# Attention over fp16 halves with weight halves kept in memory, and an output half read one step earlier

## What is computed

```python
def _L0_attn_ref(x, Wq, bq, Wk, bk, Wv, bv, Wo, bo):
    q = proj(Wq, bq) * scale          # proj: x @ W + bias, split in 16 heads
    k = proj(Wk, bk)
    v = proj(Wv, bv)
    q = apply_rotary(pos, q)
    k = apply_rotary(pos, k)
    sim = jnp.einsum('bhid,bhjd->bhij', q, k)
    sim = jnp.where(causal, -jnp.finfo(sim.dtype).max, sim)
    attn = jax.nn.softmax(sim, axis=-1)
    out = jnp.einsum('bhij,bhjd->bhid', attn, v)
    out = out.transpose(0, 2, 1, 3).reshape(b, n, INNER)
    return out @ Wo + bo
...
x = _layernorm(x + _L0_attn_ref(...), axis=-1)
x = _layernorm(x + _L0_ffn_ref(...), axis=-1)
```

## Time and profile before

| | us |
|---|---|
| median of three runs | 1857.92 (1856.61 to 1859.83) |
| the profiled execution | 1852.92 |
| its span in the profile | 1851.1 |

### The profile page before, as it was taken

How to read it: one execution, slowest core, us unless ns; L and a number is a source line. 1 busy time by engine, 2 the same in 40 slices (tenths; PEclk the granted TensorE clock), 3 DMA queues, 4 the chain that set the end, 5 groups by cost and what they waited for, 6 DMA issues and landing times. The chain is left out here.

```text
span 1851.1 us, 33747 instructions
## 1 busy us (share of the span) xinstructions
PE 1755.6 (95%) x10464; PEld 1409.7 (76%) x10464; DVE 1564.9 (85%) x3748; ACT 1463.9 (79%) x2658; POOL 1394.8 (75%) x1293
## 2 busy tenths in 40 slices
PE   6899999999999999999999999999999999899997
PEld 4677877777777777777777777777777777668886
DVE  6788888888888888988888888888888889867886
ACT  5788888888888888888888888888888888754443
POOL 4688877778777878888778878787888877624554
PEclk9899999999999999999999999999999999989999
DMA  3756565666665666576666655675666765540001
GB/s 93 165 116 113 111 139 117 122 131 129 118 119 120 142 120 115 114 157 119 120 122 117 138 111 116 141 141 121 119 114 116 156 141 109 104 99 12 24 24 35
DMA packets 638257, 210.01 MB, mean 113 GB/s; under 512 B 609408, under 2 KB 622208, under 8 KB 636672
## 3 DMA queue, kind: packets, MB, share of 16 engines
q1 hardware_dynamic: 614400, 165.91, 47.9%
q10 hardware_dynamic: 23680, 41.95, 7.9%
HBM read 48.40 MB, written 8.39 MB: 31 GB/s over the span
## 5 line engine op out<-in xcount | busy, mean ns | idle before, releaser
L863 DVE SCALAR_TENSOR_TENSOR planes<-S,recip,planes 128x128 f16<-128x128 f32 (+7 forms) x512 | 417.5, 815 | 113.0 <-ACT planes L665 111.3
L656 ACT ACTIVATE S<-p_row,neg_max 128x128 f32<-128x128 f32 (+7 forms) x512 | 381.5, 745 | 138.9 <-DVE neg_max L853 138.8
L665 ACT ACTIVATE planes<-S,recip 128x128 f16<-128x128 f32 (+7 forms) x512 | 378.9, 740 | 101.4 <-DVE recip L914 73.7
L427 POOL TENSOR_TENSOR swap<-swap,sin_t 128x512 f32<-128x512 f32 x256 | 331.5, 1295 | 166.0 <-ACT swap L673 164.9
L853 DVE CUSTOM_DVE_ANT_0 p_row<-S,mask_row 128x128 f32<-128x128 f32 (+7 forms) x512 | 387.0, 756 | 27.0 <-PE S L1123 26.4
L421 POOL TENSOR_TENSOR rot<-rot,swap 128x512 f32<-128x512 f32 x252 | 325.5, 1292 | 53.6 <-DVE rot L904 50.7
L673 ACT ACTIVATE swap<-S,bqk 64x512 f32<-64x512 f32 x512 | 350.8, 685 | 18.6 <-PE S L1141 5.8
L1123 PE MATMUL S<-QKA 128*128 128x512 f32 (+4 forms) x1152 | 261.9, 354 | 10.3 <-DVE planes L863 5.7
L1123 PE MATMUL S<-QKB 128*128 128x512 f32 (+4 forms) x1152 | 260.4, 353 | 0.4 <-DVE planes L863 0.3
L1074 PE MATMUL O<-PT,VA 128*128 128x512 f16 (+3 forms) x1152 | 215.4, 328 | 29.0 <-issue 25.5
L1074 PE MATMUL O<-PT,VB 128*128 128x512 f16 (+3 forms) x1152 | 214.9, 327 | 29.4 <-issue 27.0
(11 more groups left out here) (134 smaller groups left out, 2955.5 us busy)
## 6 DMA issues: line engine op xcount, KB each, us to landing
w_raw<-in_w_heads ACTq DMA_DIRECT2D x64, 256.0 KB, 2.9
wv_raw<-in_w_heads ACTq DMA_DIRECT2D x32, 256.0 KB, 3.4
PT<-planes SPq DMA_TRANSPOSE x512, 3.4
wo_raw<-in_wo_heads ACTq DMA_DIRECT2D x32, 256.0 KB, 2.6
attn_d<-resid ACTq DMA_DIRECT2D x4, 1024.0 KB, 6.3
x_raw<-in_x_cols SPq DMA_DIRECT2D x3, 1024.0 KB, 5.9
resid<-in_x_rows ACTq DMA_DIRECT2D x3, 1024.0 KB, 5.3
resid<-in_x_rows SPq DMA_DIRECT2D x2, 1024.0 KB, 6.8
```

Of the source, the lines that this page charges most:

```text
L427: nc.gpsimd.tensor_tensor(swap[:, c, :], swap[:, c, :], sin_t[:, half], ALU.mult).then_inc(sin_done, 1)
L656: nc.scalar.activation(row_psum(n, s)[:, 0:cols], p_row[:, k % 2, 0:cols], ACT.Exp, bias=neg_max[:, s:s + 1], scale=-1.0, accum_out=row_su ...
L665: nc.scalar.activation(row_halves(n, s)[:, 0], row_psum(n, s)[:, 0:cols].rearrange("p (j q) -> p j q", q=P), ACT.Copy, scale=recip[:, s:s ...
L863: nc.vector.scalar_tensor_tensor(halves_of[:, 1], row_psum(n, s)[:, 0:cols].rearrange("p (j q) -> p j q", q=P), recip[:, s:s + 1], halves_ ...
```

## The change

- x, W, WV, QK, OT and WO become fp16 halves (`at(...)` places them by hand in one region, so that the later part's float32r operands can lie over them). Since fp16 has a narrow range, each gets a factor from a bound: x a factor per batch, W of each head, WV and WO of each pair. The maxima are VectorE's (`weigh_w`, `weigh_v`, `weigh_wo`), their sum over partitions is a matmul with ones read by `take_...`, and `scale_...` makes the factors and what undoes them: the biases `bqx`, the factor `to_score` of the masked maximum, which was the constant -SCALE, `v_up`, and `pv` of the addition into resid. The raw weights are multiplied by GpSimd before they are split.
- The halves of the weights of heads 0 to 15 are written to memory once (`keep_...` on SyncE), and from head 16 on they are loaded into `W`, `WV` and `WO` as they are (`load_..._halves`); weighing, copying and subtracting weights ends with head 15. At each change of batch the factors are renewed (`weigh_all`, `take_x`, `scale_x`, `scale_out`).
- `w_raw`, `wv_raw` and `wo_raw` have two buffers, `WV` and `WO` too. In heads 1 to 13 `w_high` stands in steps 1 and 2.
- `output_high` and `output_low` of the second half of O stand in step 6.
- The loads of resid and x and the stores of resid are cut into quarters, one or two to a step.

The core of the diff:

```diff
-    xT = sb("xT", [P, 2, KT, N], F32R)
...
+    xT = at(AT_X, "xT", [P, 2, KT, N])
+    W = [at(AT_W + 4096 * i, f"W{t}", [P, 2, 2, KT, P]) for i, t in enumerate("AB")]
+    WV = [at(AT_WV + 2048 * i, f"WV{t}", [P, 2, KT, 2, P]) for i, t in enumerate("AB")]
+    QK = [at(AT_QK + 16384 * i, f"QK{t}", [P, 2, 2, N]) for i, t in enumerate("AB")]
+    OT = [at(AT_OT + 8192 * i, f"OT{t}", [P, 2, N]) for i, t in enumerate("AB")]
+    V = [sb(f"V{s}", [P, 2, NT, 2 * P], F16) for s in "AB"]
+    WO = [sb(f"WO{s}", [P, 2, 2, DIM], F16) for s in "AB"]
...
+            def keep_w(m):
+
+                sp.wait_ge(w_lo, n_w(m, 1))
+                sp.dma_start(w_d[m], W[m % 2][:, :, :, :, :].rearrange("p q a t c -> p (q a t c)")).then_inc(w_kept[m % 2], 16)
+
...
 
             def turn(n, s):
 
@@ -407,13 +505,11 @@
...
+            def w_scale(m):
+
+                pool.wait_ge(wq_scaled, 5 * m + 2)
+                raw = w_raw[m % 2][:, :, :, :].rearrange("p q t c -> p (q t c)")
+                nc.gpsimd.tensor_scalar(raw, raw, sw[:, m:m + 1], None, ALU.mult).then_inc(w_up, 1)
+
...
+            def load_w_halves(m):
+
+                act.wait_ge(chunked, n_four(m - 2, 3))
+                for i in range(2):
+                    act.wait_ge(w_kept[i], n_two(H - 2 + i))
+                act.dma_start(W[m % 2][:, :, :, :, :].rearrange("p q a t c -> p (q a t c)"), w_d[m % H]
+                              ).then_inc(w_loaded[m % 2], 16)
...
-                    if s == 7 and prev:
+                    if s == 6 and prev:
...
+                    if n == 0 and s in (2, 3):
+                        w_high(2, s - 2)
+                    if 1 <= n < H - 2 and s in (1, 2):
+                        w_high(n + 2, s - 1)
...
-                nc.scalar.activation(OT[q][:, 0, o], O[:, :], ACT.Copy, scale=pv_down[:, slot:slot + 1]
+                nc.scalar.activation(OT[q][:, 0, o], O[:, :], ACT.Copy, scale=1.0 / UP
...
+            def weigh_w(m):
+
+
+                dve.wait_ge(W_in[m % 2], n_two(m))
+                wait(dve, wq_summed, m - 1)
+                nc.vector.tensor_reduce(wq_max[:, m % 2:m % 2 + 1], w_raw[m % 2][:, :, :, :].rearrange("p q t c -> p (q t c)"),
+                                        AX.X, ALU.max, apply_absolute_value=True).then_inc(wq_abs, 1)
+
+            def take_w(m):
+
+
+                dve.wait_ge(wq_summed, m + 1)
+                ts(gw[:, m:m + 1], w_sum(m), 1e-9, 1.0 / UP, ALU.max, ALU.mult).then_inc(wq_scaled, 1)
+
+            def scale_w(m):
+
+                one = slice(m, m + 1)
+                dve.wait_ge(wq_scaled, 5 * m + 1)
+                nc.vector.reciprocal(sw[:, one], gw[:, one]).then_inc(wq_scaled, 1)
+                dve.wait_ge(x_scaled, 2)
+                ts(one_x[:, :], gw[:, one], gx[:, 0:1], None, ALU.mult).then_inc(wq_scaled, 1)
+                dve.wait_ge(wq_scaled, 5 * m + 2)
+                ts(bqx[:, 0, :, m], bqk[:, :, m], sx[:, 0:1], sw[:, one], ALU.mult, ALU.mult).then_inc(wq_scaled, 1)
+                dve.wait_ge(wq_scaled, 5 * m + 3)
+                stt(to_score[:, 0, one], one_x[:, :], -SCALE / DOWN ** 2, one_x[:, :], ALU.mult, ALU.mult
+                    ).then_inc(wq_scaled, 1)
...
+            def scale_wo(pair):
+
+                one = slice(pair, pair + 1)
+                dve.wait_ge(wo_scaled, 3 * pair + 1)
+                nc.vector.reciprocal(so[:, one], go[:, one]).then_inc(wo_scaled, 1)
+                nc.vector.tensor_tensor(pv[:, 0, one], bu[:, 0, one], go[:, one], ALU.mult).then_inc(wo_scaled, 1)
+
...
             def masked_scores(n, s):
...
                 nc.vector.tensor_tensor_reduce(row_view(p_row[:, k % 2, 0:cols], s),
                                                score_view(row_psum(n, s), s), row_view(mask_row[:, N - cols:], s),
-                                               -SCALE, -MASKED, ALU.add, ALU.min,
+                                               to_score[:, n // H % 2, n % H:n % H + 1], -MASKED, ALU.add, ALU.min,
                                                neg_max[:, s:s + 1]).then_inc(maxed, 1)
 
...
-                nc.vector.tensor_tensor(into, into, X[:, :], ALU.add).then_inc(added, 1)
+                pair = (n - 2) // 2
+                if pair < H // 2:
+                    dve.wait_ge(wo_scaled, 3 * pair + 3)
+                else:
+                    dve.wait_ge(out_scaled, pair // (H // 2))
+                stt(into, X[:, :], of_pair(pv, pair), into, ALU.mult, ALU.add).then_inc(added, 1)
```

666 lines of the change are left out of this document (465 added, 201 removed).

## The result

The changed kernel takes **1844.77 us** (median of 5 runs, 1840.99 to 1849.04); the kernel before, run beside it, 1856.61 us (5 runs, 1853.11 to 1859.83). The ratio is 0.9937 with a 95% interval of 0.9913 to 0.9962: **12 us less, 0.6%**. I had forecast 1829 us, 28 less. The direction held and the time lies in the range; the size is less than half of what I summed. The profiled execution of the changed kernel is the longest of its five, so some of what its trace loses is its own.

The account below looks back on a forecast made before the run. The VectorE-ScalarE chain was taken to bound the kernel. Terms -48 + 21 - 5 + 4 = -28 us took the profiled 1852.9 to 1825; the median stands 5 us above: 1829 us (55%), range 1775 to 1862.

Parts of the forecast that it names:

- What bounds the kernel: In mid-attention the chain between VectorE and ScalarE sets the pace; VectorE waits for TensorE's scores only 26.4 us in all.
- Moving the read of O: Reading O's second half in step 6 instead of 7 changes the chain by 0, bounds -0.4 and +0.4 us a head.
- Heads 16 to 63: Per pair: scores -0.86, weighing -1.2, WO's copy -0.6, pointer operands +0.66; sum -2.0 us, over 24 pairs -48 us.
- Heads 0 to 15: Weighing and copying stay, W's copies and scale work are added: +3.5 us a pair, over 6 pairs +21 us.
- Start: Maxima of x and W cost about 4 us, mostly hidden behind WV's load; two later ScalarE waits ease: -5 us.
- Batch changes: At three batch changes, six small instructions and two GpSimd passes over x add +1.5 us each, +4 us.
- GpSimd's fp16 forms: GpSimd's casts and subtractions in attention, untraced with fp16, were taken as unchanged; the subtraction stays at 1285 ns.
- rival 4: GpSimd's fp16 casts and subtractions become slower and bound the heads; at twice their durations 1935 us; chance 8%.
- Rival 1: Pointer operand costs nothing and small instructions of heads 0 to 15 fall into waits: 32 us less, 1797 us; chance 22%.
- Rival 2: TensorE's whole relief shows in all 64 heads, 3.0 us each: 1665 us; chance 2%.
- Rival 3: All new work of heads 0 to 15 is in the chain, 48 us against 48 saved: 1857 us; chance 8%.
- Rival 5: TensorE, idle for 8% instead of 3%, gets a lower granted clock; at 0.85 in attention 1920 us; chance 5%.

## Why the forecast was right or wrong

**Where the size was lost.** The sum said -28 us and the traces show -3.9. Two terms account for the difference: the start, +9.4 instead of -5, and the batch changes, +7.1 and +6.0 instead of +1.5 each. The term for heads 16 to 63 came out near by luck. Each is taken up below.

**What bounds the kernel** was right for the even head and wrong for the odd one. The step that failed is "TensorE is hardly what the others wait for". I took the 26.4 us of VectorE's waiting for scores as the whole of TensorE's influence. It was only the part shown under that name: ScalarE's waits for maxima held more of it, and fell by 75 us when TensorE got its room (20 of them came back as waits for reciprocals).

**Moving the read of O: 0.** Wrong for the edit alone (-1.31 us a pair, -22 us in all), and right within its bounds for the edit inside this change (0.17 a pair). The step that failed is pricing each part against the kernel before. Moving TensorE's wait, shortening what it computes and shortening what VectorE does in step 5 relieve one place; the first relief is paid in full, the others in part (0.17 for 1.31, 0.38 for 1.26).

**Heads 16 to 63: -2.0 us a pair.** Measured -2.39. The operand: +0.66 foretold, +0.44 measured for the maxima; the additions into resid weren't tried apart. The weights' share: -1.8 foretold, -1.26 alone and -0.38 behind the move. The form: -0.86 foretold, -1.14 as the last step. The sum came near because the move, put at nothing, and the weights' share, put too high, make up for each other. That is luck.

**Heads 0 to 15: +3.5 us a pair.** Measured 3.0 to 3.3 in heads 2 to 7: right as a sum, and the maxima over W and WO are hidden as I assumed (less than 0.05 us a head without them). The other parts weren't tried apart, and the move, which I had at nothing, gives 0.6 us a pair here in the kernel before, so the rest of the new work may cost more than I summed. Heads 9 and 11 cost 2 and 3 us more; the second is the maxima over x, which the change moves there from head 13, behind those over W and WO.

**Start: -5, bounds -9 and +5.** Measured +9.4 at head 2, outside the bounds, and the largest miss. The step that failed is "so little of the 4 us shows". The 4 us were 6.7, the load that ScalarE's queue held before gave back 3.5 of them, and 3.2 showed. What I didn't price at all is the new work behind the first chunk, 6.6 us up to the first maximum; 3.9 of it is where TensorE's sums stand, in front of the second chunk. Of the two later waits that I credited, one went: ScalarE waited 4.85 us for a weight, and head 0 is 3.5 us shorter without it (25.11 to 21.61). The other stayed, 3.3 us of the 3.7, and head 1 is 3.1 us longer (28.11 to 31.25). So 9.8 - 3.5 + 3.1 = 9.4. Before and after:

```profile
46.95 0.80 ACT L665 ACTIVATE planes<-S,recip 128x640 f16<-128x640 f32 x1 [4.85 <-POOL WA L458]
71.59 0.47 ACT L843 ACTIVATE planes<-S,recip 128x256 f16<-128x256 f32 x1 [3.32 <-DMA PT<-planes]
```

**Batch changes: +1.5 each.** Measured 7.1 and 6.0 us for the second and third, when each is held against the same heads of the kernel before. The reload of the residual, which the change only cuts up and moves to earlier steps, makes a transposed row land late (3.7 and 3.2 us here, and in most executions, not all). The maxima over x moved to a head with no slack for them (1.5). The small scale instructions cost 2.0 instead of a few tenths, since two of them wait until GpSimd's instruction ends. The step that failed is the count of "six small instructions and two passes" by their own durations, which leaves out what they wait for and what moves with them.

**GpSimd's fp16 forms:** the row decides against rival 4, with a gain instead of a loss, 1158 ns for 1285. The Trainium skill's rule ("GPSIMD Engine Reference", § 3, the per-element model), held by the read port and not by bytes, would have left 1285; the trace is 10% below it. Hardly anybody waited for these 0.13 us: where weight loads wait for that half, it is 6.9 us in all.

**Rivals.** Rival 1 (more hidden) fell with the 0.44 us that the operand costs. Rival 2 (TensorE's whole relief) has the right engine, for two fifths of its size: with the read moved and the form changed 1.31 + 1.14 us a pair came, not 6, and the 1.14 hold what else comes with the form. Rival 3 (nothing left) is nearest in time, 1857 us, for another reason: not the first batch but start and batch changes ate the gain. Rival 5 (the clock) did not happen in the steady state, with 1.00 in 1000 to 1050 us, in the stretch of the result above. It did happen in small. Between 85 and 1580 us the kernel after has five short stretches at the 1.2 GHz level, behind waits of TensorE of 2.7 to 3.3 us; the kernel before has none. The mean granted clock of the whole is 0.985 against 0.991. That costs TensorE 11 us at most (an estimate: 0.006 of 1847 us), and part of it is in the lengths of the late heads above.

## What to carry to other kernels

Price the parts of a change in the order in which they would be made, and ask after each what bounds the step now: two reliefs of one engine don't add. If one edit is a line long and takes a wait off an engine that is busy for 97%, run it alone first; here it beat the change that contained it. Where work moves once per batch or to the start, look up what else stands in that step, DMA queue included: about half of the loss here was work that already existed, in a new place.

## What the runs showed of the hardware

- **A VectorE instruction of 8 elements took 1.30 us** because GpSimd was in the middle of one, and two such in a row each waited for one of GpSimd's. The kernel before had it too: its 128x2 products took 0.16 to 1.23 us, its copies into 128x128 0.21 to 1.32. I had priced the new small ones by 147 ns.
- **GpSimd scales slowly:** 512 elements in place by a [128, 1] operand took 1566 to 1621 ns, where a cast of 512 takes 613 and a subtraction 1158. It isn't the operand: 1024 elements took 2.85 us with it, and 2.78 and 3.19 with a constant.
- **A [128, 1] operand in place of a constant costs VectorE 0.06 us** in all three forms seen: maximum (689 to 749 ns), addition (684 to 750) and, taken away, reading O (746 to 686). Only the trial of the maximum changes nothing else; the addition changed its operation with it, and the read of O the type of its result.
- **The granted clock fell behind a single wait.** TensorE waited 3.2 us, until 288.1; over the next stretch the clock averaged 0.86, so a part of it ran at the lower of the two levels, 1.2 GHz. There two groups of three matmuls like each other in all took 0.84 and, a little later, 0.49 us. Pauses up to 1.9 us in the steady state left it at 1.00, and so did a single one of 3.58 us, until 424.05:

```profile
284.00:290.00 6.00, 2.81 (x17) 1.54 (x15) 5.87 (x12) 4.23 (x9) 5.08 (x6) 0.95 0.96 127
290.00:300.00 10.00, 10.00 (x58) 6.67 (x56) 8.77 (x26) 6.00 (x11) 9.89 (x10) 0.86 0.29 62
424.00:434.00 10.00, 9.95 (x61) 5.94 (x62) 7.69 (x23) 9.78 (x20) 7.28 (x6) 1.00 0.53 114
```

```profile
289.42 0.84 PE L1460 MATMUL X<-WOB,OTA 128*128 128x256 f16 x3
298.09 0.49 PE L1460 MATMUL X<-WOB,OTA 128*128 128x256 f16 x3
```

- **Transposing DMAs issued within 4 us of two loads (256 and 512 KB) landed 10.1 to 12.8 us after their issue,** four of them in heads 32 and 48, against a median of 3.8 us in the same execution. With the same loads in other steps none of the 512 took over 7.9 us.
